# Routing roots by Newton's method on DVE, six shared parts held for the first border, and the last attention period's statistics at its beginning

## The reference, cut to what matters

```python
x = x + 0.5 * ffn(layernorm(x))      # layer 0
x = x + attention(layernorm(x))
x = x + 0.5 * ffn(layernorm(x))      # layer 1

def ffn(x):                          # per token
    scores = softmax(x @ gate_w.T)   # 16 experts in 4 groups
    # two best groups by the sum of their two best scores, then the two best experts
    y = sum(weight[e] * expert[e](x) for e in chosen)
    z = silu(x @ ws1 + bs1) * (x @ ws3 + bs3) @ ws2 + bs2   # shared expert
    return y + z

def layernorm(x): return (x - mean(x)) / sqrt(var(x) + 1e-5)
```

## Time and profile before

| what | us or share |
|---|---|
| median of three runs (lowest, highest) | 1244.09 (1242.54, 1245.39) |
| the profiled execution: its own time | 1243.24 |
| its span | 1241.5 |
| PE busy | 1148.4 (93%) |
| DVE busy | 852.7 (69%) |
| ACT busy | 759.6 (61%) |
| POOL busy | 698.1 (56%) |
| mean granted clock of PE | 0.982 |

### The profile page before, as it was taken

The page is one execution under the profiler, slowest core; times in us unless marked ns, Lnnn a source line. Parts: engine busy times, 40 slices in busy tenths (PEclk is TensorE's granted clock), DMA queues, the critical chain, the costliest instruction groups (busy, mean ns, idle before and its releaser), DMA issues.

```text
span 1241.5 us, 26349 instructions
## 1 busy us (share of the span) xinstructions
PE 1148.4 (93%) x6696; PEld 904.6 (73%) x6696; DVE 852.7 (69%) x2774; ACT 759.6 (61%) x1698; POOL 698.1 (56%) x850
## 2 busy tenths in 40 slices
PE   7988999999999967899998999889998999999995
PEld 5555555899999946777887878545557999999653
DVE  6788784566666655768878786677844666666488
ACT  4454441688888845675655653544415888888398
POOL 3577776488888854000411503356763888887810
PEclk9999999999999998999999999899999999999997
DMA  9922227556555523012320400114585555555398
GB/s 360 309 91 95 98 104 201 172 172 174 171 172 156 164 104 105 32 38 68 112 72 24 133 22 35 35 69 141 171 210 180 173 170 174 173 157 162 119 400 333
DMA packets 94215, 181.53 MB, mean 146 GB/s; under 512 B 17624, under 2 KB 60400, under 8 KB 92022
## 3 DMA queue, kind: packets, MB, share of 16 engines
q1 hardware_dynamic: 66630, 110.44, 29.2%
q0 software_dynamic: 26016, 67.55, 15.3%
q10 hardware_dynamic: 1424, 1.86, 0.5%
HBM read 97.63 MB, written 86.08 MB: 148 GB/s over the span
## 4 chain that ended last, share of the span: by engine, by line
PE 58%; DVE 17%; ACT 11%; issue 5%; POOL 5%; DMA 3%; SPq 1%; DVEq 0%; ACTq 0%; POOLq 0%
PE bank L700 20%; PE bank L710 10%; PE bank L559 7%; PE bank L691 5%; POOL expert_rows L1683 4%; PE bank L575 4%; PE bank L806 3%; ACT rows L1021 3%; ACT w L1021 3%; DVE stat L1161 2%; PE bank L756 2%; PE bank L732 2%; ACT xn L1039 1%; PE bank L521 1%; ACT rows L898 1%
## 5 line engine op out<-in xcount | busy, mean ns | idle before, releaser
L700 PE MATMUL bank<-rows,att 128*128 128x128 f32 x2288 | 303.2, 276 | 0.3 <-ACT att L1010 0.3
L700 PEld LDWEIGHTS bank<-rows,att 128*128 128x128 f32 x2288 | 279.2, 192 | 0.8 <-ACT att L1010 0.6
L1683 POOL DMA_INDIRECT expert_rows<-rows,slots x160 | 155.4, 971 | 80.0 <-issue 57.3
L1010 ACT COPY att<-w 128x512 f32 x286 | 177.0, 619 | 10.2 <-issue 4.2
L1740 POOL DMA_INDIRECT routed_rows<-silu,rdest x160 | 158.3, 989 | 35.0 <-issue 24.6
L1458 DVE SCALAR_TENSOR_TENSOR rows<-bank,tile_b,att 128x128 f32<-128x128 f32 x286 | 100.1, 350 | 112.9 <-ACT att L1015 102.0
L710 PE MATMUL bank<-w,rows 128*128 x572 | 171.5, 382 | 4.3 <-DVE rows L1458 4.2
L1740 POOL DMA_INDIRECT routed_rows<-rows,rdest x126 | 124.7, 990 | 68.4 <-DVE rdest L1441 40.7
L1009 ACT COPY rows<-bank 128x256 f32<-128x256 f32 x286 | 106.6, 373 | 89.1 <-PE bank L691 86.9
L575 PE MATMUL bank<-ws,be 128*128 128x256 f32 x512 | 124.0, 388 | 8.6 <-DVE be L1364 8.6
L925 ACT ACTIVATE silu<-bank,bs 128x512 f32<-128x512 f32 x64 | 43.9, 686 | 127.6 <-PE bank L559 117.5
(11 more groups left out here) (212 smaller groups left out, 2156.9 us busy)
## 6 DMA issues: line engine op xcount, KB each, us to landing
rows<-expert_rows SPq DMA_DIRECT2D x286, 129.5 KB
rows<-routed_rows SPq DMA_DIRECT2D x32, 512.0 KB, 4.2
w<-routed_rows SPq DMA_DIRECT2D x10, 1024.0 KB, 10.9
out<-xres SPq DMA_DIRECT2D x16, 512.0 KB, 9.3
xres<-in_x SPq DMA_DIRECT2D x7, 1024.0 KB, 9.5
rows<-routed_rows SPq DMA_DIRECT2D x6, 1024.0 KB, 7.7
expert_rows<-pad SPq DMA_DIRECT2D x47, 129.5 KB, 14.0
w<-in_w SPq DMA_DIRECT2D x1, 4096.0 KB, 24.4
```

Of the source, the lines that this page charges most:

```text
L700: last = nc.tensor.matmul(rh_ps[t % RB][:, n * P:(n + 1) * P], m.rw13[:, t % RB, c * C + n * INTER:c * C + (n + 1) * INTER], m.rT[:, t % R ...
L1010: nc.scalar.copy(m.rw13[:, a % RB, :].rearrange("p (c n) -> p c n", c=KC), w13[:, :, bass.ds(expert_at(i + 2), C)]).then_inc(s.rw13_copied, 1)
L1683: nc.gpsimd.indirect_dma_start(out=d.xg, out_offset=bass.IndirectOffsetOnAxis(ap=m.slots[:, slots_of(r), k, i:i + 1], axis=0), in_=m.xs[bu ...
```

## The change

Three things change, and the counts that follow from them.

- For batches 3 to 7 of layer 0 and 6 and 7 of layer 1 (r = 3 to 7, 14, 15) the root is computed on DVE: a shift of the bits, a subtraction from a constant, and Newton steps (`approach_root`, three more steps of the generator, with 10 operations, behind the statistics), of which the last operation stands in `negate_mean`. GpSimd's `rstd` for these batches goes. DVE's steps for each shared part follow from 17 + 7 instead of 17 + 4 where statistics are in the period. The other roots of routing and attention stay on GpSimd.
- Parts 41, 43 and 45, all of batch 7, are held for the first border beside 44, 46 and 48. There ACT does the silu of part 46 behind the weighing, and DVE's order is written anew: three gatings, then combines with the first two additions between them, the fourth gating behind the statistics, the last two additions behind `a_negate_mean`.
- In the last attention period the statistics of r = 13 are taken behind those of r = 11, at the beginning, and counted on a semaphore of their own.

```diff
@@ module @@
-HELD = ((44, 46, 48), (29, *range(31, PARTS)))
+HELD = ((41, 43, 44, 45, 46, 48), (29, *range(31, PARTS)))
-UPS, DOWNS = (4 * 7 + 2, 4 * 13), (PAIRS * 7 + 2, PAIRS * 13)
-HELD_UP, HELD_DOWN = ((7, 2), (13, 0)), ((7, 1), (13, 0))
+UPS, DOWNS = (4 * 7, 4 * 13), (PAIRS * 7, PAIRS * 13)
+HELD_UP, HELD_DOWN = ((7, 0), (13, 0)), ((7, 0), (13, 0))
+def rooted_by_dve(r):
+    return 3 <= r < BATCHES or r > NEXT + 2
@@ scalar @@
-            for n in HELD[0]:
+            for n in HELD[0][0:3]:
                 shared(0, n)
-
             for h in range(PAIRS):
                 weigh_routed(0, h)
+            for n in HELD[0][3:]:
+                shared(0, n)
@@ vector @@
+            def error_of_root():
+                ch.then(TT(m.root_by[:], m.root, m.ve[:], ALU.mult))
+                ch.then(nc.vector.scalar_tensor_tensor(m.root_err[:], m.root_by[:], -0.5, m.root, ALU.mult, ALU.mult))
+            def better_root(out):
+                return nc.vector.scalar_tensor_tensor(out, m.root_err[:], 1.5, m.root, ALU.add, ALU.mult)
+            def approach_root(ready):
+                dve.wait_ge(s.stats_ready, ready)
+                ch.then(nc.vector.tensor_scalar(m.half_bits[:], m.ve[:].bitcast(I32), 1, None, ALU.arith_shift_right))
+                ch.then(nc.vector.tensor_scalar(m.root_bits[:], m.half_bits[:], -1.0, float(0x5f3759df), ALU.mult,
+                                                ALU.add))
+                for _ in range(2):
+                    error_of_root()
+                    ch.then(better_root(m.root))
+                    yield
+                error_of_root()
+                yield
...
             def negate_mean(r):
                 own = tiles_of(r)
-                dve.wait_ge(s.rstd_ready, r + 1)
-                wait(dve, s.xn_half, normalised_of(r))
+                if rooted_by_dve(r):
+                    wait(dve, s.xn_half, normalised_of(r))
+                    ch.then(better_root(own.rstd[:, :]))
+                else:
+                    dve.wait_ge(s.rstd_ready, r + 1 - 5 * (r >= BATCHES))
+                    wait(dve, s.xn_half, normalised_of(r))
@@ vector, stats_work @@
                 aggregate(s.stats_ready)
                 yield
+                if rooted_by_dve(r):
+                    yield from approach_root(r + 1 - (r > NEXT + 2))
@@ vector, add_shared @@
-                if r == BATCHES - 1 and p == 2:
+                if r == BATCHES - 1 and p == 0:
                     dve.wait_ge(s.bias_added, 1)
@@ vector, route @@
-                        shared(L, n + 1 + j, work, (17 + 4 * ahead) // others + 1)
+                        shared(L, n + 1 + j, work, (17 + 7 * ahead) // others + 1)
@@ vector, border @@
-            for n in HELD[0]:
-                shared(0, n, iter(()), 0)
-
-            for h in range(PAIRS):
+            for u in range(3):
+                gated(BATCHES - 1, u)
+            for h in range(2):
+                combine(0, h)
+                add_shared(BATCHES - 1, h)
+            for h in range(2, PAIRS):
                 combine(0, h)
             aggregate(s.a_stats_ready)
+            gated(BATCHES - 1, 3)
             a_negate_mean(0)
+            for p in range(2, PAIRS):
+                add_shared(BATCHES - 1, p)
@@ vector, last attention period @@
                 else:
-                    route_stats(BATCHES + EARLY)
+                    route_stats(NEXT)
+                    stats(NEXT + 2 - BATCHES, range(NT), m.early)
+                    aggregate(s.later_stats, m.early)
...
-                if not more:
-                    route_stats(NEXT + 2)
@@ gpsimd @@
             def rstd(r):
-                pool.wait_ge(s.stats_ready, r + 1)
+                if r == NEXT + 2:
+                    pool.wait_ge(s.later_stats, 1)
+                else:
+                    pool.wait_ge(s.stats_ready, r + 1 - (r > NEXT + 2))
@@ gpsimd, route @@
                     scatter(r, 0)
-                    if r != NEXT and b + 3 < BATCHES:
-                        rstd(r + 3)
                     scatter(r, 1)
-                    if r == BATCHES + EARLY:
-                        rstd(r + 3)
```

More of the change, by code:

```diff
@@ L139, in allocate @@
     m.nmr = sb("nmr", [P, NT])
+    m.half_bits = sb("half_bits", [P, NT], I32)
+    m.root_bits = sb("root_bits", [P, NT], I32)
+    m.root = m.root_bits[:, :].bitcast(FP32)
+    m.root_by = sb("root_by", [P, NT])
+    m.root_err = sb("root_err", [P, NT])
     m.mx = sb("mx", [P, NT])
@@ L323, in program @@
     s.spare_out, s.setup_done = sem("spare_out"), sem("setup_done")
+    s.later_stats = sem("later_stats")
     s.stats_ready, s.rstd_ready, s.nmr_ready = sem("stats_ready"), sem("rstd_ready"), sem("nmr_ready")
```

## The result

The changed kernel takes 1251.14 us (median of 9 runs, 1248.10 to 1253.98) where the kernel before takes 1244.09 beside it: a ratio of 1.0052, 95% interval 1.0036 to 1.0069. That is 6 to 7 us slower. The forecast was 1250.4, its sum +6.3 us. The profiled execution took 1253.53 us with a span of 1251.8.

The account below looks back on a forecast made before the run. DVE's selection was taken to bound layer 0's four-part routing periods, GpSimd's scatters the five-part ones by about 1.1 us. Terms 8.6 + 0 - 2.3 = +6.3 us on 1243.24 gave 1249.5, as a median 1250.4; range 1240.5 to 1255.0.

Parts of the forecast that it names:

- The root's price and place: Layer 0 routing: 2.26 us a root on DVE; +0.8 to batch 1's ranking, +3.52 each to batches 2's and 4's.
- The wait on scatters goes: Five-part periods, to the rankings of batches 3 and 5: PE's wait on GpSimd's scatters ends, -1.1 us each.
- Cold stretches: Layer 0: PE's stops ahead of the rankings of batches 2 and 4 bring half clock, +1.5 us each, +3.0.
- Sum to the experts: Layer 0 up to the experts: 0.8 + 7.0 - 2.2 + 3.0 = +8.6 us.
- The border: First border, three more held parts: PE's idle 16.20 us holds them, transposes may come warm; 0, bounds -0.3 and +2.
- Layer 1: Moved statistics -3.5, cold stretch gone -1.5, unhidden at period's start +0.7, four-part period's root +2.0: -2.3 us.
- The period with a root: Layer 1's four-part routing period ending at 837.60: DVE-bound and already with the late selection, +2.0 us.
- Rival 1: GpSimd is the bound and DVE takes the roots in idle time: 1237.6 us, faster; chance 0.20.
- Rival 2: Selection late as forecast, but PE's clock does not fall: 3.0 us less, 1247.4; chance 0.20.
- Rival 3: Selection later by the roots alone, gating and add fit ahead, clock stays: 1244.9 us, no change; chance 0.14.
- Rival 4: As forecast, and PE comes cold into experts and border, 1.5 us each: 1253.4 us; chance 0.06.
- The rule of the Trainium skill: GpSimd and DVE share an SBUF port: up to 1.7 us back per four-part period, the sum 3.4 less.

Follow-up runs that it names:

- run 3: Changed kernel with ten steps more instead of seven beside the parts, so DVE's selection comes ahead of the gating again: 1245.98 us, ratio 1.0012 to the kernel before.
- run 4: Changed kernel with the root's ten operations moved behind the choices, and four steps: 1243.21 us, ratio 0.9988 to the kernel before.
- run 5: Changed kernel with only the roots of batches 3, 5 and 7 on DVE, the others on GpSimd: 1241.38 us, ratio 0.9972 to the kernel before.
- run 2: Kernel before with the roots alone moved to DVE, held parts and statistics as before: 1256.97 us, ratio 1.0100 to the kernel before.
- run 6: Kernel before with the moved statistics alone: 1241.33 us, ratio 0.9962 to the kernel before; timed again 1239.05 us, ratio 0.9959.
- run 7: Kernel before with the six held parts and the border's new order alone: 1243.74 us, ratio 0.9983 to the kernel before.
- run 8: Changed kernel with three held parts and the border's old order: 1252.69 us, ratio 1.0066 to the kernel before.
- run 1: Changed kernel with all routing roots back on GpSimd, held parts and moved statistics kept: 1241.02 us, ratio 0.9968 to the kernel before.

## Why the prediction was right

**The root's price and place** (2.26 a root; +0.8 at R1; +3.52 for each of R2 and R4). The ten operations took 2.08 us for an assumed 2.05 in the period to R3, and R1 moved by 0.64. The two four-part periods grew by 4.01 each, 0.5 more than the step. Part of that can be read in DVE's timeline ahead of R2: from `ve` (L1180) to the softmax's sum it takes 2.42 us instead of 0.08, since the sum had overlapped `ve` and the shift took 0.38; with 0.19 for the eleventh operation and 1.26 for the order that is 3.8 of 4.0. The stop I had put at some 4 us ahead of the ranking is split, 2.50 us ahead of a down (the gating that PE waits for there stands behind the root, too; it was 1.00 before, which I hadn't counted) and 2.93 ahead of the ranking. The mechanism, a late selection behind gating and add, is shown by run 3.

**The wait on scatters goes, -1.1 in each five-part period.** The wait did go: the changed kernel has none, and runs 4 and 5 together show that the pows of batches 4 and 6 made it. The price was too low rather than too high: the period to R5, at full clock, fell by 1.60, beyond my bound of 1.4. The four-part period ahead, longer by 4 us, gave GpSimd room as well, and the two aren't told apart here. The period to R3 rose by 0.16, since it has the fall of the clock behind R2 in it.

**Cold stretches, +1.5 for each long stop.** The price was right: 1.5 by the change beside run 2, 1.6 by the two timings of run 6. The number was not. Behind R2 the clock was 0.66 in 84 to 89 as expected. For R4 it fell within the period instead, behind the stop at 124.90, where DVE sets the pace, and was full behind the ranking. So layer 0 paid some 1.5 us where I had 3.0. Where in the period the clock falls is luck: run 2, with the same routing 0, fell behind R4. Sum to the experts: +8.6 forecast, +7.9 measured at be2's add, from four-part periods 1.0 above, and five-part periods with their falls 2.2 below, what I had, and 0.65 more behind R5.

**The border, 0 (-0.3 to +2).** The changed kernel showed +1.6, within the bounds, but the sign of my argument was wrong: I had PE come warm to the transposes. It did (1.04 us for eight instead of 1.94), and yet they are later, since they queue behind a down that takes 6.69 us at half clock after a stop of 6.96. PE had been idle 16 us there before as well, with nothing queued ahead of the transposes. In the time of the whole kernel this loss doesn't show (runs 7, 8).

**Layer 1, -2.3.** The statistics gave -2.85 at the first transposes and -1.5 up to the next ranking, as the step had it (-3.5 - 1.5 + 0.7). The period with a root gave +4.2 instead of +2.0: eight ups behind 816.97 take 5.37 us, so the cold stretch that I had counted as gone has moved here. Run 1 has it without the root, and its period is 27.86 us, 1.75 longer than before; the root adds 2.45. The period to 871.54 holds the root of batch 7, which I had at nothing, and takes 24.26 us instead of 22.38, so 1.9 more, of which a longer cold stretch has a part (gate scores 1.94 us instead of 1.07). Between two traces with a full clock there the root's share shows better: 22.38 us with that root (run 3, PE waiting 1.14 us for the selection), 20.71 without (run 6, second timing). By be2's add layer 1 had lost 2.2 us where I had 2.3 gained, and this step failed in two terms: the cold stretch was moved and not removed, and the second root wasn't free. The experts of layer 1 took 1.7 back; DVE waits 4.45 us for be2 instead of 6.33, but why they are shorter wasn't looked into.

**What made the total come out** at +7 for +6.3 is thus partly luck. In the profiled execution there are errors of opposite sign (layer 0 0.7 too high, border and layer 1 too low), the two spans differ by 10.3 us, and the medians lie some 3 us closer together than they do; the profiled execution of the changed kernel is the second slowest of nine. The decision between the cases was right for its own reason: the slower sign comes from the selection in the four-part periods. Rival 1 (GpSimd the bound, 1237.6) fell with R2, 4.65 us later, and with run 1. Rival 2 (no fall of the clock) fell with the windows: in the thirteen traces of this case each stop of PE of 3.4 us or more behind the first 50 us was followed by a stretch below 1.00, and only shorter ones went either way (run 6). Rival 3 (roots alone) fell with run 3. Rival 4 (cold into experts and border as well) was half right: cold at the border, and cold behind PE's 10.54 us of waiting for rows at 226.84 (0.50 over the next 5 us), but there DVE waits 3.68 us for be2, so PE doesn't set the pace.

The rule of the Trainium skill that was weighed ahead (Perfetto Trace Analysis, "Optimizing Scalar/DVE Operations": a port shared by GpSimd and DVE) would, as the prediction used it, have given 3.4 us back in the four-part periods. No run shows that: with the pows gone the selection still takes 0.29 us (132.07), and these periods grew by more than the step for root and order.

## What to carry to other kernels

Before work is moved to an engine "with idle time", look where in that engine's order it lands: two us of small dependent operations on a vector engine that is 70% busy cost 4 us in each period that waits for it and about 2 in the period of layer 1 that had no other wait to hide it (24.26 instead of 22.38). When yields are added to hand-interleaved work, count anew how many steps are handed out per part; here the missing ones were half of the loss (run 3). When a part is tested by itself, ask which wait it stands in: run 5 moved the roots that nobody waited behind. Edits that come together are to be timed apart: the moved statistics were worth 2 to 5 us and went under in the roots' 10.

## What the runs showed of the hardware

A stop of PE of 2.3 to 3 us was enough for a stretch at 1.2 GHz in several places, but not always. Stops of 2.50 and 2.93 us ahead of R2 in the changed kernel were followed by a clock of 0.66; a stop of 2.95 in run 3 with a second one of 1.24 ahead of R2 (82.93) was followed by a full clock, and one of 2.93 in the same kernel (123.10) by 0.76. One kernel took 22.35 us for a period in one execution, with a fall, and 20.71 in another, without (run 6). After a fall, eight ups took 5.1 to 6.6 us instead of 3.6. I had counted one fall per long stop; in layer 1 the kernel with a shorter stop at the beginning simply fell at the next one.

A chain of 128x8 operations on DVE costs 0.20 us each for some 0.17 of duration, and now and then one (the shift or the magic constant) takes 0.28 to 0.42 us.
